# A decoder layer on one core: the front half of each attention slot runs one slot earlier, with three buffers for the probabilities

## What is computed

```python
x = x + self_attn(_layernorm(x))            # causal
x = x + cross_attn(_layernorm(x), ctx, ctx) # then @ Wc.T + bc
x = x + ffn(_layernorm(x))                  # softmax of logits, groups, top 6, experts, shared
# in both attentions:
attn = softmax(scores, axis=-1)             # exp(s - max(s)) / sum
out  = attn @ v
```

## Time and profile before

| | us |
|---|---|
| median of 3 runs | 716.64 |
| lowest, highest | 714.97, 718.74 |
| the profiled execution | 718.88 |
| its span | 717.0 |
| TensorE matmul busy | 639.0 |
| VectorE busy | 471.2 |
| GpSimd busy | 341.0 |
| ScalarE busy | 332.8 |

### The profile page before, as it was taken

How to read it: one execution, slowest core, us unless ns; L and a number is a source line. 1 busy time by engine, 2 the same in 40 slices (tenths; PEclk the granted TensorE clock), 3 DMA queues, 4 the chain that set the end, 5 groups by cost and what they waited for, 6 DMA issues and landing times. The chain is left out here.

```text
span 717.0 us, 16771 instructions
## 1 busy us (share of the span) xinstructions
PE 639.0 (89%) x6161; PEld 450.4 (63%) x6161; DVE 471.2 (66%) x1278; ACT 332.8 (46%) x634; POOL 341.0 (48%) x374
## 2 busy tenths in 40 slices
PE   1599999999888889988998989899999999999991
PEld 0256666666667666666775445467787778667761
DVE  3157676757878798989896579925455455445463
ACT  2367777776766776776664442222222222222000
POOL 6012321121354443445412256487777777777473
PEclk9899999999999999999999999999999999999996
DMA  8222333343444321332131159239999999844597
GB/s 247 38 45 46 85 83 83 89 101 83 72 109 109 79 66 35 86 75 53 32 99 38 45 155 252 85 94 223 255 250 269 249 249 268 222 76 67 123 358 264
DMA packets 144705, 94.27 MB, mean 131 GB/s; under 512 B 62192, under 2 KB 142320, under 8 KB 144624
## 3 DMA queue, kind: packets, MB, share of 16 engines
q1 hardware_dynamic: 129008, 74.58, 39.7%
q0 software_dynamic: 10240, 14.16, 10.6%
q10 hardware_dynamic: 5376, 4.46, 1.9%
HBM read 60.26 MB, written 24.50 MB: 118 GB/s over the span
## 5 line engine op out<-in xcount | busy, mean ns | idle before, releaser
L1443 POOL DMA_INDIRECT sum_d<-tk,targets x64 | 91.9, 1435 | 29.9 <-issue 14.4
L790 DVE TENSOR_REDUCE mx<-Sc 128x16 f32<-128x1024 f32 x64 | 78.2, 1222 | 36.5 <-PE Sc L434 36.2
L1263 PE MATMUL Sc<-xT,wgu_sb 128*128 128x96 f32 (+1 forms) x768 | 92.8, 271 | 0.0
L658 ACT COPY ET<-ring 128x512 f32<-128x512 f32 x128 | 68.9, 589 | 41.1 <-PE ring L446 38.4
L1263 PEld LDWEIGHTS Sc<-xT,wgu_sb 128*128 128x128 f32 (+1 forms) x768 | 87.2, 187 | 0.4 <-issue 0.4
L462 PEld LDWEIGHTS O<-vbd,ET 128*64 128x64 f32 x2048 | 66.6, 138 | 29.2 <-issue 17.0
L794 DVE TENSOR_TENSOR E<-Sc,mx 128x1024 f32<-128x1024 f32 x64 | 78.4, 1225 | 6.9 <-DVE mx L790 0.5
L446 PE MATMUL ring<-ident,E 128*128 128x128 f32 x512 | 69.5, 279 | 11.9 <-ACT E L697 11.9
L1436 POOL DMA_INDIRECT rows<-rows_d,tokens x64 | 64.2, 1003 | 29.1 <-issue 13.1
L462 PE MATMUL O<-vbd,ET 128*64 128x34 f32 x2048 | 73.6, 225 | 3.2 <-ACT ET L658 2.7
L434 PE MATMUL Sc<-kbd,qT 64*64 64x256 f32 x1024 | 71.9, 384 | 5.0 <-DMA kbd<-kT 5.0
(11 more groups left out here) (208 smaller groups left out, 1195.1 us busy)
## 6 DMA issues: line engine op xcount, KB each, us to landing
wgu_sb<-in_wgu_dram SPq DMA_DIRECT2D x128, 176.0 KB, 3.6
sum_d<-zeros SPq DMA_DIRECT2D x16, 524.0 KB, 5.8
kbd<-kT SPq DMA_DIRECT2D x248, 32.0 KB, 2.2
wda_sb<-in_wd_dram SPq DMA_DIRECT2D x32, 160.0 KB
wgu_sb<-sum_d SPq DMA_DIRECT2D x10, 512.0 KB, 9.5
X<-in_x_dram SPq DMA_DIRECT2D x8, 512.0 KB, 6.5
rows_d<-xhT SPq DMA_DIRECT2D x8, 512.0 KB, 2.9
out_dram<-X ACTq DMA_DIRECT2D x8, 512.0 KB, 6.6
```

The lines of the kernel that those rows point to most:

```text
L658: nc.scalar.copy(ET[:, m % 2, 4 * v:4 * v + 4].rearrange("p j q -> p (j q)"), bank(name)[:]).then_inc(s_act, 1)
L790: nc.vector.reduce_max(mx[:, m % 2, :], sc, AX.X).then_inc(s_mx, 1)
L1263: last = nc.tensor.matmul(GP[e % 2][0:m, CAP * u:CAP * (u + 1)], wgu_cols[j][:, c, m0:m0 + m], xT[:, e % 2, c, :], start=c == 0, stop=c == 1)
L1443: pool.indirect_dma_start(w["sums"][e % 2], bass.IndirectOffsetOnAxis(ap=targets[:, e:e + 1], axis=0), outs[:, e % OB, :], None, compute_o ...
```

## The change

In all five queues, scores, shift and exp are moved one slot ahead: TensorE's slot m now holds scores(m+2), VectorE's shift(m+2), ScalarE's exp(m+2). The pieces that prepare groups (normalize, xt, queries, keys, values, stats, deviation, bias) are moved along by one slot, by writing them with f = m + 1. Everything behind the probabilities (probs_t, probs, pv, recip, output, residual, out_t, wc) and routing stays at its slot, so the offset between the two halves grows by one slot. E_ gets a third buffer, so shift(m) now waits for the transposes of tile m-3. The loops start one slot earlier (FIRST = -13). `ring_uses` is changed in the same way as TensorE's queue. No instruction is added or removed. The core of the diff (the same f = m + 1 is put into the ring's list, and into VectorE's and GpSimd's loops):

```diff
-FIRST, LAST = -12, 2 * NT + 10
+FIRST, LAST = -13, 2 * NT + 10
...
-                        last = nc.tensor.transpose(out[:, 128 * j:128 * (j + 1)], E_[:, m % 2, at:at + 128], ident[:])
+                        last = nc.tensor.transpose(out[:, 128 * j:128 * (j + 1)], E_[:, m % 3, at:at + 128], ident[:])
...
-                if 0 <= m + 1 < 2 * NT:
-                    scores(m + 1)
+                if 0 <= m + 2 < 2 * NT:
+                    scores(m + 2)
...
-                nc.scalar.activation(E_[:, m % 2, :], E_[:, m % 2, :], ACT.Exp).then_inc(s_exp, 1)
+                nc.scalar.activation(E_[:, m % 3, :], E_[:, m % 3, :], ACT.Exp).then_inc(s_exp, 1)
...
-                if m % 4 == 3 and is_cross((m + 5) // 4):
-                    normalize((m + 5) // 4, 0)
-                    normalize((m + 5) // 4, 1)
...
+                f = m + 1
...
+                if f % 4 == 3 and is_cross((f + 5) // 4):
+                    normalize((f + 5) // 4, 0)
+                    normalize((f + 5) // 4, 1)
...
+                elif f % 4 == 3:
+                    if 0 <= (f + 5) // 4 < 2 * NG:
+                        keys((f + 5) // 4)
+                if 0 <= m + 2 < 2 * NT:
+                    exp(m + 2)
...
-                if m >= 2:
-                    dve.wait_ge(s_fill, ring.filled(("TP1", m - 2)))
+                if m >= 3:
+                    dve.wait_ge(s_fill, ring.filled(("TP1", m - 3)))
...
-                if 0 <= m + 1 < 2 * NT:
-                    shift(m + 1)
-                gp, gx, t = (m + 12) // 4, (m + 9) // 4, m % 4
+                if 0 <= m + 2 < 2 * NT:
+                    shift(m + 2)
+                f = m + 1
+                gp, gx, t = (f + 12) // 4, (f + 9) // 4, f % 4
...
-                if m % 4 == 2 and is_cross((m + 6) // 4):
-                    deviation((m + 6) // 4)
+                if f % 4 == 2 and is_cross((f + 6) // 4):
+                    deviation((f + 6) // 4)
...
-        mem["E"] = sb("E", [128, 2, H * S])
+        mem["E"] = sb("E", [128, 3, H * S])
```

More of the change, by code:

```diff
@@ L552, in _ @@
                     wc(m - 2)
-                if m % 4 == 1:
-                    if is_self((m + 7) // 4):
-                        xt((m + 7) // 4, 0)
-                    if is_self((m + 3) // 4):
-                        queries((m + 3) // 4, 1)
-                    if is_cross((m + 3) // 4):
-                        xt((m + 3) // 4, 1)
+                f = m + 1
+                if f % 4 == 1:
+                    if is_self((f + 7) // 4):
+                        xt((f + 7) // 4, 0)
+                    if is_self((f + 3) // 4):
+                        queries((f + 3) // 4, 1)
+                    if is_cross((f + 3) // 4):
+                        xt((f + 3) // 4, 1)
+                elif f % 4 == 2:
+                    if is_self((f + 6) // 4):
+                        xt((f + 6) // 4, 1)
+                    if is_self((f + 2) // 4):
+                        values_t((f + 2) // 4)
+                elif f % 4 == 3:
+                    if 0 <= (f + 5) // 4 < 2 * NG:
+                        keys((f + 5) // 4)
+                else:
+                    if is_self((f + 4) // 4):
+                        queries((f + 4) // 4, 0)
+                    if is_cross((f + 4) // 4):
+                        xt((f + 4) // 4, 0)
+                if m % 4 == 1:
                     if routed((m - 9) // 4):
@@ L563, in _ @@
                         weights_t((m - 13) // 4)
[L564 to L568 removed]
                 elif m % 4 == 3:
[L570 to L571 removed]
                     if routed((m - 7) // 4):
                         xn_t((m - 7) // 4)
[L574 to L578 removed]
+                elif m % 4 == 0:
                     if routed((m - 8) // 4):
@@ L744, in _ @@
-                if 0 <= m + 1 < 2 * NT:
-                    exp(m + 1)
-                if m % 4 == 1:
-                    if is_self((m + 3) // 4):
-                        queries((m + 3) // 4, 1)
-                    if is_cross((m + 3) // 4):
-                        xt((m + 3) // 4, 1)
+                f = m + 1
+                if f % 4 == 0 and is_self((f + 8) // 4):
+                    normalize((f + 8) // 4, 0)
+                    normalize((f + 8) // 4, 1)
+                if f % 4 == 1 and is_self((f + 7) // 4):
+                    normalize((f + 7) // 4, 2)
+                    normalize((f + 7) // 4, 3)
@@ new lines, in _ @@
+                if f % 4 == 3 and is_cross((f + 5) // 4):
+                    normalize((f + 5) // 4, 0)
+                    normalize((f + 5) // 4, 1)
+                if f % 4 == 0 and is_cross((f + 4) // 4):
+                    normalize((f + 4) // 4, 2)
+                    normalize((f + 4) // 4, 3)
+                if f % 4 == 1:
+                    if is_self((f + 7) // 4):
+                        xt((f + 7) // 4, 0)
+                elif f % 4 == 2:
+                    if is_self((f + 6) // 4):
+                        xt((f + 6) // 4, 1)
+                elif f % 4 == 3:
+                    if 0 <= (f + 5) // 4 < 2 * NG:
+                        keys((f + 5) // 4)
@@ new lines, in _ @@
+                if 0 <= m + 2 < 2 * NT:
+                    exp(m + 2)
+                if f % 4 == 1:
+                    if is_self((f + 3) // 4):
+                        queries((f + 3) // 4, 1)
+                    if is_cross((f + 3) // 4):
+                        xt((f + 3) // 4, 1)
+                elif f % 4 == 2:
+                    if is_self((f + 2) // 4):
+                        values((f + 2) // 4)
+                elif f % 4 == 0:
+                    if is_self((f + 4) // 4):
+                        queries((f + 4) // 4, 0)
+                    if is_cross((f + 4) // 4):
+                        xt((f + 4) // 4, 0)
@@ L758, in _ @@
                         xn_t((m - 7) // 4)
-                else:
-                    if is_self((m + 4) // 4):
-                        queries((m + 4) // 4, 0)
-                    if is_cross((m + 4) // 4):
-                        xt((m + 4) // 4, 0)
+                elif m % 4 == 0:
                     if routed((m - 8) // 4):
```

90 lines of the change are left out of this document (30 added, 60 removed).

## The result

The changed kernel takes 712.0 us (median of 19 runs, 707.0 to 716.5), beside 719.0 us for the kernel before (median of 19 runs, 714.9 to 721.2, and one of 1603.6 that stands far outside) on the same chips. The ratio is 0.991, with a 95% interval of 0.988 to 0.993, so the change gains 0.94%, about 6.7 us. The forecast was 709 within 705 to 716, and a gain. The profiled execution of the changed kernel has a span of 709.5 us (717.0 before).

What follows compares the result with a forecast made beforehand. TensorE was taken to set self attention's pace, key blocks to hold 195 to 240 us, VectorE the late groups. Terms 1.8 + 4.4 + 2.0 - 3.1 + 2.4 + 0.4 = 7.9 us took 716.64 to 709, range 705 to 716.

Steps and rivals of the forecast that it cites:

- lead at the first cross scores: TensorE reaches the first cross scores 8.2 us earlier: 1.79 first tile, 4.4 self attention, 1.99 less back work in front.
- late groups: Late cross groups: each of five becomes about 0.5 us shorter, 2.4 us in all, with VectorE setting the pace.
- the end: Last tile: a wait of 1.71 us goes, but route_norm and ScalarE's copies come later, leaving 0.4 us of gain.
- Self attention: Six TensorE waits of 0.73 us for the exponential, in front of the transposes of probabilities, go: 4.4 us gained.
- the first tile: TensorE's wait for the exponential in front of the first transposes of probabilities goes: 1.79 us gained.
- the rival: Self attention: pv waits for the ET copies where the transposes waited, so the 4.4 us stay; 713 us, chance 0.10.
- The loop of the key blocks: From 195 to 240 us the lead is carried unchanged; key waits near 2, 3 to 3.5 and 1.4 us.
- The clock rival: TensorE's granted clock drops at the second and third key-block waits, 1.5 us worse; 710 us, chance 0.12.
- The slot owed: Behind the key blocks' loop, the slot owed has grown by the output projection's two steps: 3.1 us of lead lost.
- ScalarE becomes the bound: Late cross groups: GpSimd delays route_norm 2.0 us, each of five loses 2.0; 721 us, chance 0.06; half: 715, chance 0.14.
- 0.9 us for the keys' bank: Late cross groups: TensorE waits about 0.9 us for the keys' bank, replacing a wait for the exponential.
- 0.8 at wc: Late cross groups: wc is held up by another 0.8 us or so, the copy of oT being behind the exponential.

Runs made afterwards that it cites:

- e1_act_late: The changed kernel with ScalarE's route_norm put behind the keys' copies and the exponential of its slot; 711.8 us, ratio 0.993 to the kernel before.
- e2_pool_swap: The changed kernel with GpSimd's route_deviation in front of the next group's deviation instead of behind it; 709.8 us, ratio 0.988 to the kernel before.
- e3_two_buf: The changed kernel with two buffers of probabilities instead of three, the slots still moved; 709.6 us, ratio 0.988 to the kernel before.
- e4_scores_only: The changed kernel with only scores, shift and exp moved ahead, the pieces that prepare groups left at their old slots; 756.4 us, ratio 1.055 to the kernel before.
- e9_early_swap: The changed kernel with the cross groups' keys one slot earlier and GpSimd's route_deviation in front of the deviation; 705.4 us, ratio 0.981 to the kernel before.

## Why the prediction was right, and where it was not

The direction and the size held: 6.7 us of gain by the runs, where the prediction had 7.6 between medians. But of its sum of 7.9 us (where five times 0.5 is put at 2.4) attention gave only 5.25, and the terms were not all right. Against the lead of TensorE's scores over the kernel before (corrected for 0.18 us of later start):

| | predicted us | measured us |
|---|---|---|
| lead at the first cross scores | 8.2 | 8.9 |
| carried to the third cross group | unchanged | unchanged, 8.9 |
| behind it, the first routed group | -3.1 | -3.4 |
| late groups, four | 2.4 (five) | 2.1 |
| the end | 0.4 | -2.4 |
| attention | 7.9 | 5.25 |

**Self attention** was right. All six waits for the exponential and that of the first tile went, and from 50 to 175 us TensorE now waits for nothing at all. Where no projection stands between transposes and product, in the last self group and the first cross ones, the product waits for ET, as the rival said: 3.8 us in seven places, which were 2.7 in six before. A group became 0.79 us shorter where 0.73 was taken. Not foreseen: at the start, a ring bank takes 0.72 of the 1.79 us back.

**The loop of the key blocks** carried the lead, as said, and the second wait is 3.43 us, where 3 to 3.5 were said. Its third is gone, where 1.4 was said. That the lead came out unchanged is in part luck. The loop's turn is not a fixed 19.4 us: without a fall of the clock the second turn took 18.74 us (e1_act_late), so about 0.7 us could have been gained there, and the clock took them back. Why a turn is shorter than before the change was not followed up. The clock rival had the event and nearly the price. Behind the second wait the granted clock fell to 0.57 over 4 us, near the lower level of 1.2 GHz, and cost 0.7 us (half of the 1.5 given for two falls). The second fall came in another place than was said, behind the 1.82 us wait outside the loop, and cost 1.1. The Trainium skill (TensorE: Matmul & The Clock Gate, the part on the HAM clock gate) has it that an idle array falls back to its throttled default. The direction agrees, but the length of a wait alone doesn't tell: behind 1.82 us the clock fell in one kernel and not in the next.

**"The slot owed", -3.1 us behind the loop, was the right number in the wrong place.** The loss of 3.4 us behind the loop has another cause. In e2_pool_swap, with the clock up in this group, only 1.1 us are lost there, and TensorE's waits for the keys' bank and oT in that slot (0.45 and 0.79) account for them; nothing is left to owe. The slot owed is paid at the end: there the lead falls by 2.4 us, from 7.6 at the last group's scores to 5.25 at the cut, and in e2_pool_swap by the same 2.4, from 10.9 to 8.6. Taken together with the end's 0.4 the prediction had -2.7 for it. That this fall is the slot owed is read from where the lead is lost; no run separates it. What it did not have is the 3.4.

**ScalarE in the first routed group**: this is the step that failed. The prediction computed the keys' copy for a late group, with route_norm's values there in time, and gave the delay by GpSimd to a rival ("ScalarE becomes the bound", 721 for the whole, 715 for half of it, in five groups). The chain did come late, by 1.32 us in the first routed group and by 0.61 in the second, but in no group behind them. By the differences of the runs above, the 3.4 us lost in the first are 1.2 for this, 1.1 for the clock that fell behind the longer wait, and 1.1 for the keys' bank and oT, which the prediction expected in the later groups only as a swap against the old waits. The split between the first two rests on e3_two_buf, under the condition given there; together they are 2.3 us in any case. GpSimd's four steps of one chain took 2.03 us (229.45 to 231.48), where 2.0 was estimated from the power's 1.04. The delay was priced right; what was missed is that it falls due at the beginning, not in all groups or none.

**The late groups** were right: 0.54, 0.69, 0.71 and 0.18 us gained, on average 0.53 for the 0.5 taken. The 0.9 us for the keys' bank is 0.70 and the 0.8 at wc is 0.79.

**The experts' phase** was taken as unchanged, and gave 2.4 us in the profiled pair by scatter. This is what brings 5.25 near the 7.5 of the spans, so in the profiled pair the close match with 7.9 is luck. The gain by the medians, 6.7 with an interval of some 5 to 8 us, can't tell the two.

## What to carry to other kernels

When the front half of a software pipeline is moved ahead, the pieces that feed it have to go too (here they decide between 1% faster and 5% slower), and each in-order queue has to be looked at where two chains now meet: an exchange of two chains on an engine that is idle half of the time gave back 1.7 us. Read the lead over the old kernel at several places of the trace, not the total: that tells a loss from a debt that is only due later, and it shows a gain that lies ahead of the edit and can't be its work. In a ring of few banks, look which engine frees the bank that a use gets: the same pieces in another order within the slot were worth 0.36 us a group.

## What the runs showed of the hardware

The clock: a wait of TensorE of 1.82 us was followed by 4 us at 0.57 in one kernel and at 1.00 in another with the same order of TensorE's work. Elsewhere 4 us at 0.57 came behind waits of 0.71 us (e1_act_late, 190 us), 2.98 and 3.43 us, and none came behind 0.69 us (the change, 190 us), 1.54 us (e1_act_late, 209 us) and 2.75 us (e4_scores_only, 102.7 us). Such a fall is worth 0.7 to 1.1 us in the attention of one run, as much as some of the effects sought here, and a part of it can be hidden in a wait that follows. Without it, and with no wait for key blocks, the same kernel repeated its attention phase to 0.03 us in 370, while a later phase of the same program varied by 3.6 us; there a difference of phases from one profile each can be sharper than that of nineteen whole runs.

On SyncE the issue alone of 16 small copies (32 KB each) makes more than half of a turn of the key blocks' loop. The rows are from e9_early_swap:

```profile
187.13 1.09 SPq L327 DMA_DIRECT2D ctxA<-in_ctx_rows_dram  x1
188.31 11.56 SPq L310 DMA_DIRECT2D kbd<-kT  x16
...
204.01 0.80 SPq L327 DMA_DIRECT2D ctxA<-in_ctx_rows_dram  x1
204.92 11.43 SPq L310 DMA_DIRECT2D kbd<-kT  x16
```

16 key blocks take 11.56 and 11.43 us here, 10.8 to 11.5 in the same two turns of the kernel before, of the change and of its first three relatives, so about 0.7 us each, while one lands 2.2 us (median) after its issue. In the kernel shown, with the keys asked for one slot earlier, that is hidden.
